# A linear attention by convolution: three kv buffers, the two heads of a pair in turn, and another order of its first loads

## The reference

```python
def xattn(k, v, q, ssm_kernel, D, head_dim):      # k = v = context, q = layernorm(x)
    B, HD, L = k.shape                            # 16, 128, 256
    k_, v_, q_ = (m.reshape(B, H, head_dim, L) for m in (k, v, q))      # H = 16, head_dim = 8
    kv = einsum('bhil,bhjl->bijhl', k_, v_)
    y = irfft(rfft(kv, n=2*L) * rfft(ssm_kernel, n=2*L), n=2*L)[..., :L]
    out = y + kv * D[None, None, None, :, None]
    out = einsum('bijhl,bhil->bjhl', out, q_)
    return out.transpose(0, 2, 1, 3).reshape(B, H * head_dim, L)
x = x + xattn(context, context, layernorm(x), ssm_kernel, D, 8)
```

## Time and profile before

| what | value |
| --- | --- |
| median of three runs | 846.27 us (844.44 to 847.44) |
| profiled execution | 844.39 us |
| its span in the trace | 842.6 us |
| first attention, to the end of its last reduction | 0 to 118.7 us |
| busy in the span: TensorE, VectorE, ScalarE, GpSimd | 87%, 67%, 38%, 55% |

### The profile page before, as it was taken

One profiled execution on the slowest core, in us unless ns is written; L12 is line 12 of the kernel. 1 busy time (PEld: TensorE's weight loads), 2 busy tenths in 40 slices (PEclk: granted clock), 3 DMA queues, 4 the chain that ended last, 5 costly groups with the idle time before them and its releaser, 6 DMA issues.

```text
span 842.6 us, 14795 instructions
## 1 busy us (share of the span) xinstructions
PE 735.3 (87%) x5249; PEld 664.8 (79%) x5249; DVE 560.5 (67%) x1348; ACT 319.9 (38%) x656; POOL 463.5 (55%) x528
## 2 busy tenths in 40 slices
PE   3899979974699998066989999999999999999996
PEld 3343339763699998055889999999999999999996
DVE  5588888779566665457766667667676676664533
ACT  2100014561266665226444434343444344433321
POOL 4788846441766661546427647466366474453532
PEclk9999985895699999568899999999999999999999
DMA  8310002494576676441401102002011010000000
GB/s 277 121 34 19 0 15 88 130 194 95 184 195 194 198 177 146 137 119 51 119 19 52 38 8 58 26 20 68 3 57 33 14 39 26 2 14 1 2 13 14
DMA packets 42296, 63.17 MB, mean 75 GB/s; under 512 B 7120, under 2 KB 31728, under 8 KB 41968
## 3 DMA queue, kind: packets, MB, share of 16 engines
q1 hardware_dynamic: 33776, 38.71, 14.1%
q0 software_dynamic: 8352, 23.47, 12.1%
q10 hardware_dynamic: 96, 0.04, 0.0%
HBM read 47.37 MB, written 14.84 MB: 74 GB/s over the span
## 4 chain that ended last, share of the span: by engine, by line
PE 42%; DVE 6%; ACT 4%; issue 4%; POOL 2%; DMA 0%; POOLq 0%; ACTq 0%; DVEq 0%
PE bank L1242 16%; PE bank L1227 8%; PE bank L1274 6%; PE bank L1288 3%; PE bank L1260 3%; PE bank L1324 2%; DVE hid_lo L1738 2%; PE bank L1301 1%; ACT att_weights L1444 1%; POOL rows_back L1512 1%; DVE att_scaled L1648 1%; ACT am_hi L1429 1%; PE bank L1362 1%; DVE am_lo L1727 1%; DVE lora_w_lo L1603 1%
## 5 line engine op out<-in xcount | busy, mean ns | idle before, releaser
L1530 POOL TENSOR_TENSOR hid<-hid,rw_sb 128x256 f32<-128x256 f32 x112 | 91.2, 815 | 154.0 <-DVE hid L1732 153.8
L1732 DVE TENSOR_TENSOR hid<-hid,bank 128x256 f32<-128x256 f32 x112 | 46.8, 418 | 125.4 <-ACT hid L1412 124.8
L1242 PE MATMUL bank<-am_hi,lora_w_hi 128*128 128x256 f32 x448 | 126.9, 283 | 3.4 <-DVE am_lo L1727 3.4
L1242 PE MATMUL bank<-am_hi,lora_w_lo 128*128 128x256 f32 x448 | 126.7, 283 | 0.0
L1242 PE MATMUL bank<-am_lo,lora_w_hi 128*128 128x256 f32 x448 | 126.6, 283 | 0.0
L1412 ACT ACTIVATE hid<-bank 128x256 f32<-128x256 f32 x112 | 42.4, 385 | 183.7 <-PE bank L1242 183.6
L826 POOL DMA_INDIRECT rows_in<-y_scratch,slot_token x80 | 76.7, 959 | 50.0 <-issue 30.2
L1242 PEld LDWEIGHTS bank<-am_hi,lora_w_hi 128*128 128x128 f32 x448 | 85.3, 190 | 3.6 <-POOL am_lo L1541 3.6
L1512 POOL DMA_INDIRECT rows_back<-slots_scratch,comb_idx x64 | 66.8, 1044 | 36.5 <-POOLq L528 20.9
L1242 PEld LDWEIGHTS bank<-am_lo,lora_w_hi 128*128 128x128 f32 x448 | 85.2, 190 | 0.0
L1242 PEld LDWEIGHTS bank<-am_hi,lora_w_lo 128*128 128x128 f32 x448 | 85.2, 190 | 0.0
(11 more groups left out here) (257 smaller groups left out, 2214.0 us busy)
## 6 DMA issues: line engine op xcount, KB each, us to landing
slots_scratch<-y_out SPq DMA_DIRECT2D x40, 256.0 KB, 2.6
lora_stage_early<-in_lora_weights SPq DMA_DIRECT2D x16, 384.0 KB, 3.8
rows_in<-in_moe_weights SPq DMA_DIRECT2D x10, 384.0 KB, 3.8
moe_w_lo<-in_moe_weights POOLq DMA_DIRECT2D x10, 384.0 KB, 6.2
stage<-in_moe_weights SPq DMA_DIRECT2D x8, 384.0 KB, 5.5
x_sb<-in_x SPq DMA_DIRECT2D x4, 512.0 KB, 5.3
ctx_t<-in_ctx_t SPq DMA_DIRECT2D x2, 1024.0 KB, 7.6
y_scratch<-moe_y SPq DMA_DIRECT2D x8, 256.0 KB, 2.2
```

Source lines behind the costliest of these rows:

```text
L1242: last = nc.tensor.matmul(x_banks[F % 2][:, w * GT:(w + 1) * GT], wp, ap, start=False, stop=(half == 1 and k == 2), skip_group_check=True)
L1530: nc.gpsimd.tensor_tensor(f[:, F % 2, k, :], f[:, F % 2, k, :], rw_sb[:, F // FB % 2, k, :], ALU.mult)\
L1732: nc.vector.tensor_tensor(f[:, F % 2, k, :], f[:, F % 2, k, :], x_banks[F % 2][:, GT:2 * GT], ALU.mult)\
```

## The change

- kv gets three buffers, used in turn. GpSimd waits for the convolution of step n-3 before it writes kv(n), and no longer for that of step n-2.
- The steps go in another order: two heads at a time, and for each chunk the two heads in turn: (head 0, chunk 0), (head 1, chunk 0), (head 0, chunk 1), (head 1, chunk 1), (head 2, chunk 0) and so on. The PSUM bank pair is n mod 2.
- SyncE loads x quarters 0 and 1 and the context of chunk 0 ahead of its wait for the padded kernel, and behind it the first Toeplitz part, x quarters 2 and 3 and the context of chunk 1. Each chunk has its own counter.
- ScalarE asks for the kernel and D without waiting for the zeroed tile; the memset leaves out the columns that the load writes.

```diff
+KV_SLOTS, CONV_SETS = 3, 2
+CONV_ORDER = [(h, c) for first in range(0, HEADS, 2) for c in range(CHUNKS) for h in (first, first + 1)]
...
-    kv = sb("kv", [P, 2, HALVES, PAIRS])
+    kv = sb("kv", [P, KV_SLOTS, HALVES, PAIRS])
...
-            for i in range(QUARTERS):
+            def load_x(i):
                 sp.dma_start(x_sb[:, 4 * i:4 * i + 4, :], x_rows[:, 4 * i:4 * i + 4, :]).then_inc(x_loaded[i], 16)
+
+            def load_context(c):
+
+                tokens = slice(c * CHUNK_B * SEQ, (c + 1) * CHUNK_B * SEQ)
+                for h in range(HALVES):
+                    sp.dma_start(ctx_t[:, h, tokens], a["ctx_t"][h, :, tokens]).then_inc(ctx_loaded[c], 16)
...
+            load_x(0)
+            load_x(1)
+            load_context(0)
             sp.wait_ge(kpad_stored, 16)
             load_toeplitz(0)
-            for h in range(HALVES):
-                sp.dma_start(ctx_t[:, h, :], a["ctx_t"][h]).then_inc(ctx_loaded, 16)
+            load_x(2)
+            load_x(3)
+            load_context(1)
...
-            nc.gpsimd.memset(kpad[:, :], 0.0).then_inc(kpad_zero, 1)
+            nc.gpsimd.memset(kpad[:, 0:P - 1], 0.0)
+            nc.gpsimd.memset(kpad[:, P - 1 + DIM:KPAD], 0.0).then_inc(kpad_zero, 1)
...
-            pool.sem_inc(conv_done, CHUNKS)
-            pool.wait_ge(ctx_loaded, 16 * HALVES)
-            for h in range(HEADS):
-                if h % 2:
-                    k, n = h // 2, W_ORDER[h // 2]
+            for n, (h, c) in enumerate(CONV_ORDER):
+                if n % 4 == 2:
+                    k = n // 4
                     pool.wait_ge(hi_split, k + 1)
...
-                for c in range(CHUNKS):
-
-                    pool.wait_ge(conv_done, CHUNKS * h + c + 1)
...
+                if n < CHUNKS * 2 and n % 2 == 0:
+                    pool.wait_ge(ctx_loaded[c], 16 * HALVES)
+                if n >= KV_SLOTS:
+
+                    pool.wait_ge(conv_done, n - KV_SLOTS + 1)
...
-            act.wait_ge(kpad_zero, 1)
             act.dma_start(kpad[:, P - 1:P - 1 + DIM], a["ssm_kernel"]).then_inc(k_loaded, 16)
             act.dma_start(d_col[:, :], a["D"]).then_inc(k_loaded, 16)
+            act.wait_ge(kpad_zero, 1)
             act.wait_ge(d_added, 1)
...
+                pe.wait_ge(kv_ready, n + 1)
+                if n >= CONV_SETS:
+
+                    pe.wait_ge(prod_ready, HALVES * (n - CONV_SETS + 1))
```

More of the change, by code:

```diff
@@ L155, in conv_phase @@
         x_loaded = [sem(f"x_loaded{i}") for i in range(QUARTERS)]
-        ctx_loaded, ident_done = map(sem, ("ctx_loaded", "ident_done"))
+        ctx_loaded = [sem(f"ctx_loaded{c}") for c in range(CHUNKS)]
+        ident_done = sem("ident_done")
         stats_done, mv_done, rstd_step = map(sem, ("stats_done", "mv_done", "rstd_step"))
@@ L240, in _, with turn_queries @@
         def _(pe):
-            pe.wait_ge(ident_done, 2)
-            for n in range(TILES // 2):
+            def turn_queries(n):
                 pe.wait_ge(y_ready, n + 1)
@@ L250, in _, with conv @@
                 last.then_inc(q_transposed, 1)
-            for h in range(HEADS):
+            def conv(n):
+                h, slot, banks_of = CONV_ORDER[n][0], n % KV_SLOTS, n % CONV_SETS
                 for part, (first, _) in enumerate(TOEPLITZ_PARTS):
@@ L254, in _ @@
                         pe.wait_ge(toeplitz_loaded[part], 16)
-                for c in range(CHUNKS):
-                    n = CHUNKS * h + c
-                    pe.wait_ge(kv_ready, n + 1)
-                    if h >= 1:
-                        pe.wait_ge(prod_ready, HALVES * (n - CHUNKS + 1))
-                    same, across = toeplitz[:, h, 0:P], toeplitz[:, h, P:2 * P]
-                    nc.tensor.matmul(conv_banks[2 * c][:, :], same, kv[:, c, 0, :], start=True, stop=True)
-                    nc.tensor.matmul(conv_banks[2 * c + 1][:, :], across, kv[:, c, 0, :], start=True, stop=False)
-                    nc.tensor.matmul(conv_banks[2 * c + 1][:, :], same, kv[:, c, 1, :], start=False,
-                                     stop=True).then_inc(conv_done, 1)
+                pe.wait_ge(kv_ready, n + 1)
+                if n >= CONV_SETS:
+                    pe.wait_ge(prod_ready, HALVES * (n - CONV_SETS + 1))
+                own, both = conv_banks[2 * banks_of:2 * banks_of + 2]
+                same, across = toeplitz[:, h, 0:P], toeplitz[:, h, P:2 * P]
+                nc.tensor.matmul(own[:, :], same, kv[:, slot, 0, :], start=True, stop=True)
+                nc.tensor.matmul(both[:, :], across, kv[:, slot, 0, :], start=True, stop=False)
+                nc.tensor.matmul(both[:, :], same, kv[:, slot, 1, :], start=False, stop=True).then_inc(conv_done, 1)
+            pe.wait_ge(ident_done, 2)
+            for n in range(TILES // 2):
+                turn_queries(n)
+            for n in range(len(CONV_ORDER)):
+                conv(n)
         @block.vector
@@ L290, in _ @@
             dve.wait_ge(q_copied, TILES // 2)
-            for n in range(HEADS * CHUNKS):
-                h, c = n // CHUNKS, n % CHUNKS
-                dve.wait_ge(conv_done, CHUNKS + n + 1)
+            for n, (h, c) in enumerate(CONV_ORDER):
+                dve.wait_ge(conv_done, n + 1)
                 query = [q_t[:, m, :].rearrange("p (b t) -> p b t", t=SEQ)[
```

20 lines of the change are left out of this document (10 added, 10 removed).

## The result

The changed kernel takes 844.31 us (median of 20 runs, 841.98 to 844.83), the kernel before 846.74 beside it (20 runs); the ratio is 0.9964, with a 95% interval of 0.9955 to 0.9973. By the ratio that is a gain of 3.0 us (the two medians differ by 2.4) where 9.6 were forecast, and the time lies above the range of 833 to 840. The profiled execution took 843.61 us, its span is 841.9. A repetition on a second chip gave 842.35 and a ratio of 0.9947 [0.9925, 0.9968], 4.5 us.

The account below looks back on a forecast made before the run. In the first attention no engine is full, TensorE comes first and stalls for kv. Terms -7.5 (stalls), -0.3 (kv(2) earlier) and -1.8 (clock) sum to -9.6 us: 834.8 from the profiled time, 836.7 from the median, forecast 836.5, range 833 to 840.

Parts of the forecast that it names:

- seven stalls of 1.07 us: First attention, steps from 2 on: the third buffer removes all of TensorE's waits for kv, -7.5 us.
- slower: Rival, 3%: GpSimd without rests beside VectorE makes each kv operation longer; at 1.27 us the time is 849.
- the late x costs nothing, with 1.4 us of cover: Start: late x quarters move step 0 to 22.6, steps 0 and 1 end at 27.9, before kv(2) at 29.3.
- the start is late: Rival, 7%: x behind the Toeplitz load runs at 139 GB/s, block 0 and kv(2) come 4.8 us later; 841.5.
- The clock: Ahead of step 2: TensorE's idle time shrinks from 3.33 to 1.4 us, so full clock follows, -1.8 us.
- a few tenths: Rival that the clock still falls, 22%: low clock in step 0 costs this; low from step 2 on gives 838.5.
- sum of -9.6: Whole change: -7.5 for the stalls, -0.3 for kv(2) earlier, -1.8 for the clock, in us.
- 0.43 earlier: Start: the load of D and the chain behind it, to SyncE's Toeplitz load, move this many us earlier.
- Half loads: Rival, 3%: half loads do not overlap, each added transfer pays its own time, 4 us on block 0; 840.7.
- Everything after it is behind a barrier and moves with it: Behind the first attention: the rest of the kernel shifts by the whole gain of -9.6 us.

Follow-up runs that it names:

- two slots: The changed kernel with two kv buffers instead of three; 884.33 us, ratio 1.0061 to the kernel before on its chip.
- kv behind the queries: The changed kernel, but GpSimd waits with its first kv until VectorE has normalized all of x; 875.06 us, ratio 0.995 to the kernel before.
- x first: The changed kernel with all four x quarters and the first context half ahead of SyncE's wait, kv at once; 837.93 us, ratio 0.9885 to the kernel before.
- the kernel asked for at once: The kernel before with only ScalarE's load of the padded kernel not waiting and the memset sparing the middle; 845.53 us, ratio 0.999.
- split early: The changed kernel with all x and first context half ahead of the wait, kv behind normalizing, weight splits ahead of step 4k+2; 839.32 us, ratio 0.9907.
- after: The changed kernel itself, first measurement, against the kernel before; 844.31 us, ratio 0.9964.
- end delayed: The changed kernel with four memsets on VectorE at the end of the first attention; 845.96 us, ratio 1.0 to the kernel before.

## Why the prediction was wrong

*Right: the third buffer.* The forecast was seven stalls of 1.07 us, -7.5, GpSimd faster than TensorE at 2.575 us a step, VectorE following. The stretch of the changed kernel shows it (77.41 us with no wait), two slots give the stalls back (8.5 us at the next phase), and the buffer alone makes the kernel 7.2 us faster. A kv operation takes 1.005 us in a row of six (6.03 / 6); the 1.27 that the case "slower" needs is far off. The order of two heads in turn: no wait, as forecast.

*Wrong: "the late x costs nothing, with 1.4 us of cover".* This is the step that failed. The forecast had step 0 at 22.6; it started at 26.77, 4.2 later, from two errors of about the same size:

- x quarter 2 was read at 15.45 for 13.6: +1.85. The forecast let the loads behind the Toeplitz load flow at 381 GB/s from 11.6 us on. The stretches of the changed kernel show 104, 124, 198, 302 and 388 GB/s in the five microseconds from 10:

```profile
11.00:12.00 1.00, 0.62 (x3) 0.21 (x2) 0.00 (x0) 0.73 (x2) 0.00 (x0) 1.00 1.02 124
12.00:13.00 1.00, 0.00 (x0) 0.00 (x0) 0.00 (x0) 0.24 (x1) 0.00 (x0) 1.00 0.83 198
13.00:14.00 1.00, 0.00 (x0) 0.00 (x0) 0.00 (x0) 0.00 (x0) 0.00 (x0) 1.00 0.94 302
```

 By these rates the 0.79 MB of the first Toeplitz part and of quarter 2 were in at about 14.15 (an estimate), 1.15 later than the 13.0 of the forecast, and VectorE read them 1.3 behind that, where 0.6 was taken; that is the other 0.7. The kernel before has a slow rise too, with the context behind the same load: 134, 143, 302 and 412 GB/s in the four microseconds from 10. The mean of 139 over the first two hides that the third was still rising.

 The rival "the start is late" had this at 139 GB/s for 1.05 MB; its direction was right and its size too large.
- The last four normalizing operations took 3.91 for 1.52 us: +2.4. This wasn't in the forecast, nor in a rival. Moving the context forward made kv operations fall beside them. The contention was looked for on the other side only: the rival "slower" asked what VectorE does to kv in the steady state, where the products read PSUM, and missed what kv does to VectorE at the start. Two experiments separate the causes: kv behind the queries, with late x, gives 1.52 us, and x first, with early x, 3.91 us.

The cover itself was mis-sized too. The forecast held kv(2) at 29.3 while the queries moved; but ScalarE casts block 0 behind its last copy of queries, so kv(2) moved with them, to 32.2. Even with steps 0 and 1 at full clock step 2 could not have started before about 32.2.

*The clock, moved and not removed.* Full clock from step 2 on was right, and gave its 1.8 us against the first trace of the kernel before, but not for the stated reason: there was no idle time of 1.4 us ahead of step 2, since step 1 ran into it. And the 1.8 belongs to that one trace: in the second trace of the kernel before, and with the kernel asked for at once, step 2 has full clock already and step 0 the lower one. But the 1.2 GHz level fell on step 0 instead: steps 0 and 1 take 6.49 us, not 5.3, +1.2 (of it 1.1 beyond the time at which kv(2) is ready). The rival named this possibility and priced it at "a few tenths", since it would have been hidden in the cover; with the cover gone it counted nearly in full.

Together: 4.2 + 1.2 - 1.4 of cover = 4.0. The last product ends at 110.67 where 106.6 was forecast, 4.07 later. The sum of -9.6 becomes -5.5, and the next phase in the first pair of traces did start 5.49 earlier.

*Wrong without harm: the lead of the kernel.* "0.43 earlier" was 0.8 at the landing of D, and nothing at the Toeplitz load (9.20 and 9.13 for 9.10). The store takes 3.4 us from issue to landing where it took 2.5. In three traces that wait ended at 9.10 to 9.20 with 2.10 MB queued ahead of it, whether the store was issued at 5.60, 5.80 or 6.56; with 3.15 MB queued (x first, split early) it ended at 9.86 and 10.28. The store seems to be held up by the loads that were queued before it; this is read from the traces, and wasn't tried by itself. It does not wait for all of them: in the x-first version they still flow at 365 GB/s from 10 to 11 us, when the wait has ended at 9.86.

*Half loads.* Four of them queued flow at 388 to 390 GB/s once the rate is up (15 to 20 us), and no time of their own is seen in each; that rival stays down: where ScalarE waits only for it, block 0 is cast at 25.20 with the half loads (kv behind the queries) and at 24.84 to 25.40 with the whole ones. The fit that the prediction quotes from the Trainium skill stands on its page "DMA: Bandwidth & Descriptors" in another section, on the anatomy of one DMA, and there for transfers issued by GpSimd; SyncE issues these. Whether the slow rise belongs to the Toeplitz load, or to x rows beside it, is open; in the x-first version, with no x behind it, the rate is also low (179, 95 and 184 GB/s in the three microseconds from 11), so x is not needed for it.

*From -5.5 to -3.0.* "Everything after it is behind a barrier and moves with it" held for 0.83 of a shift over ten pairs, and the pair on which the forecast was measured is the one farthest from that line. The gains at the next phase in two pairs of traces are 5.49 and 3.20, 4.3 on average; the two measured gains are 3.0 and 4.5, by their ratios. The 4.8 us that the rest took longer in the first pair are, for the most part, no cost of the change: they would leave 0.7 us of the 5.49, and the 3.0 of the second pair 0.2 of the 3.20, while the runs show gains of 3.0 and 4.5, and a delay of 4.3 us at the barrier comes out as 3.6. Single traces differ in where the granted clock falls, and runs of one kernel spread over 2 to 8 us. The changed kernel's own two measurements differ by 2 us in the median, with mean granted clocks of 0.927 and 0.934. Whether the slope is below 1, and why, stays open, and with it up to a third of the gain.

## What to carry to other kernels

A transfer that is moved forward moves forward what consumes it as well: list what the freed consumer will then run beside, and on which ports, before a move is priced at zero. When a change bundles a fix of the steady state with a new start, price the start by its chain (data, statistics, normalizing, transposes, first step), each at the time it will then have; 1.4 us of cover is little for a chain of five links. The same contention cost time with late x and none with x first, so it counts by the cover that it meets. A chain taken as fixed, as kv(2) was, has to be checked for links that the moved chain also uses. And run by itself the one part that removes the measured stall: here it gave 7.2 us, and the bundle 3.0 and 4.5.

## What the runs showed of the hardware

- *VectorE is held up by GpSimd on some operations.* Four 128x256 fp32 normalizing operations from SBUF to SBUF take 1.52 us alone and 3.91 beside kv operations, in the five traces in which they meet (after, its repetition, end delayed, two slots, x first); the rows of one line in the first of these (count, shortest/median/longest ns) against the same line in the kernel before:

```profile
L307 DVE TENSOR_SCALAR y<-x_sb,meanvar,rstd x4: 770/1124/1127, 21.9 to 24.7; 128x256 f32<-128x256 f32 x4
```

```profile
L286 DVE TENSOR_SCALAR y<-x_sb,meanvar,rstd x4: 405/412/416, 17.3 to 18.5; 128x256 f32<-128x256 f32 x4
```

 A normalizing operation lasts about as long as a kv operation here (1.12 and 1.08 us at the median), as if the two took turns, while the four kv operations lose little, 4.17 for 4.03. VectorE's products from PSUM (1.29 for two, beside kv and behind the last of it) and its reductions from SBUF are not slowed beside kv:

```profile
L328 DVE TENSOR_REDUCE q_t<-prod x48: 674/676/677, 39.8 to 99.6; 128x64 f32<-128x512 f32 x48
```

 The Trainium skill, page "SBUF — State Buffer", section "SBUF: two separate sides", says that VectorE and GpSimd share one pair of ports as an exclusive lock: an operation of VectorE in a two-port mode, or with two inputs in SBUF, and one of GpSimd wait for each other whole. The trace agrees with the lock: the normalizing operation waits, and the reduction (one input in SBUF) and the product (one of its two inputs in PSUM) don't. Which of the two conditions the normalizing operation meets, the rows don't say; besides x it reads a mean and a factor per partition, from SBUF too. The forecast could have had the meeting from that page; its size, 2.4 us, is from the trace.
- *A store behind queued loads lands late.* 2.5 and 3.4 us from issue to landing for the same 24 KB, issued at 6.56 and 5.80, and 3.5 between issue and the end of SyncE's wait when issued at 5.60; see above.
- *One kernel's runs follow the mean clock.* On one chip the kernel before took 842.22 us in a run whose mean granted clock was 0.939, and 846.8 to 848.3 in its six runs at 0.925 to 0.927; the changed kernel took 837.24 at 0.943. A single pair of traces can therefore differ by as much as 5 us for another reason than the change. Where the 1.2 GHz level fell at the start also differed between two traces of the same kernel: at step 2 behind an idle time of 3.33 us, or at step 0.
